# Attention block on one core: turned tiles kept in quarter order, two small tiles normalised on GpSimd, new orders

## The reference, cut to what matters

```python
# x: (4, 512, 256); H=16 heads of E=128, KV=4 key/value heads, G=4
xn = layernorm(x)
Q = (xn @ Wq + bq); K = (xn @ Wk + bk); V = (xn @ Wv + bv)
scores = einsum('blhe,bmhe->bhlm', Q, K) / sqrt(128)   # causal mask added
attn = softmax(scores)
ctx = einsum('bhlm,bmhe->blhe', attn, V)
y = gelu(ctx @ Wo + bo)
s = layernorm(xn + y) * gamma + beta
g = silu(ffn(xn))          # gate/up 256 -> 2x1024, silu(gate)*up, down to 256
out = x + s * g
```

## Time and profile before

| what | value |
|---|---|
| median of 3 runs | 708.92 us |
| the profiled execution, its own time | 708.16 us |
| span of the profiled execution | 706.4 us |
| mean granted TensorE clock | 0.956 |
| busy in the span: TensorE, VectorE, ScalarE, GpSimd | 89%, 71%, 60%, 36% |
| DMA: share of the 16 engines | 68.3% |
| data moved | 121.35 MB in 130870 packets |

### The profile page before, as it was taken

How to read it: one execution, slowest core, us unless ns; L and a number is a source line. 1 busy time by engine, 2 the same in 40 slices (tenths; PEclk the granted TensorE clock), 3 DMA queues, 4 the chain that set the end, 5 groups by cost and what they waited for, 6 DMA issues and landing times.

```text
span 706.4 us, 10602 instructions
## 1 busy us (share of the span) xinstructions
PE 625.7 (89%) x3342; PEld 532.6 (75%) x3342; DVE 503.5 (71%) x1119; ACT 421.4 (60%) x1023; POOL 255.9 (36%) x211
## 2 busy tenths in 40 slices
...
GB/s 254 139 82 30 61 89 59 31 1 113 222 177 204 233 198 227 194 214 170 247 163 208 235 205 242 194 196 190 238 193 237 197 203 232 187 208 225 201 143 30
DMA packets 130870, 121.35 MB, mean 172 GB/s; under 512 B 16256, under 2 KB 112640, under 8 KB 128768
## 3 DMA queue, kind: packets, MB, share of 16 engines
q1 hardware_dynamic: 130128, 120.37, 68.3%
...
q10 hardware_dynamic: 688, 0.33, 0.2%
...
## 4 chain that ended last, share of the span: by engine, by line
PE 41%; DMA 29%; DVE 10%; SPq 6%; ACT 6%; issue 4%; POOL 2%; DVEq 0%; ACTq 0%; POOLq 0%
PE bank L925 13%; DMA probs<-p_scratch 11%; DMA i_scratch<-inv 9%; DMA p_scratch<-probs 8%; PE down_ps L925 6%; PE down_ps L965 6%; PE bank L954 6%; PE bank L952 6%; SPq L455 5%; DVE probs L864 4%; PE down_ps L1039 4%; ACT probs L651 3%; DMA raw<-in_wgu 2%; POOL pT_lo L532 2%; ACT pT_hi L659 1%
## 5 line engine op out<-in xcount | busy, mean ns | idle before, releaser
L532 POOL TENSOR_TENSOR pT_lo<-probs,pT_hi 128x512 fp32r<-128x512 f32 x160 | 203.4, 1296 | 341.0 <-ACT pT_hi L659 340.4
L659 ACT ACTIVATE pT_hi<-probs 128x512 fp32r<-128x512 f32 x160 | 95.3, 624 | 120.3 <-DMA probs<-p_scratch 99.0
L651 ACT ACTIVATE probs<-probs,least 128x512 f32<-128x512 f32 (+3 forms) x256 | 140.4, 552 | 4.9 <-DVE least L851 4.9
L851 DVE CUSTOM_DVE_ANT_0 probs<-bank,mask 128x512 f32<-128x512 f32 (+3 forms) x256 | 115.7, 485 | 11.8 <-PE bank L925 10.9
L864 DVE STREAM_TRANSPOSE probs<-probs 128x2048 f32<-128x2048 f32 (+1 forms) x64 | 95.7, 1496 | 21.5 <-ACT probs L651 21.5
L925 PE MATMUL down_ps<-pT_lo,v_hi 128*128 128x512 f32 x160 | 69.5, 434 | 45.3 <-POOL pT_lo L532 45.1
L1039 PE MATMUL down_ps<-wo_lo,cT_hi 128*128 128x256 f32 x256 | 74.6, 291 | 10.4 <-DVE cT_lo L883 10.4
L878 DVE TENSOR_TENSOR down_ps<-down_ps,inv_b 128x512 f32<-128x512 f32 x64 | 68.8, 1075 | 16.9 <-DMA inv_b<-i_scratch 8.7
L870 DVE SCALAR_TENSOR_TENSOR qT_lo<-bank,bias,qT_hi 128x512 fp32r<-128x512 f32 x64 | 47.7, 746 | 44.9 <-ACT qT_hi L645 44.5
L925 PEld LDWEIGHTS down_ps<-pT_lo,v_hi 128*128 128x128 f32 x160 | 31.4, 196 | 61.4 <-POOL pT_lo L532 58.3
L1039 PE MATMUL down_ps<-wo_hi,cT_lo 128*128 128x256 f32 x256 | 73.0, 285 | 0.0
...
## 6 DMA issues: line engine op xcount, KB each, us to landing
p_scratch<-probs SPq DMA_DIRECT2D x16, 1024.0 KB, 5.2
...
```

Source lines behind the costliest of these rows:

```text
L532: nc.gpsimd.tensor_tensor(lo[:], turned(t)[:, j], f32(hi[:]), ALU.subtract).then_inc(probsT_split, 1)
L651: nc.scalar.activation(p, p, ACT.Exp, bias=least[:, u, g:g + 1], scale=-1.0, accum_out=total[:, n * T + t, g:g + 1]).then_inc(exp_done, 1)
L659: nc.scalar.activation(pT[(pair_no - 1) % PT_BUFFERS][0][:], turned(t)[:, j], ACT.Copy).then_inc(probsT_hi, 1)
L851: nc.vector.tensor_tensor_reduce(out=blocks_view(t)[:, g], in0=ps[:, 0:(t + 1) * P].rearrange("p (k i) -> p k i", i=BLOCK), in1=mask[:, (T ...
```

## The change

1. Keys in quarter order. For t > 0 the score product reads its keys as `(q j i)` and not as `(j q i)`: first the keys of quarter 0 of every block of 128, then quarter 1, and so on. A unit's turned tile is then read back in runs of (t+1)·512 bytes in place of 512 bytes, still with four DMAs of 32 partitions. `ph` and `pl` read four separate runs of 128 columns where they read 512 columns in a row. The mask has a copy for each tile (128x1280 in place of 128x512) and is loaded after the last weight is split.
2. For tiles 0 and 1 (`NORMED`) GpSimd multiplies the probabilities with the reciprocals in place (new steps `no0`, `no1`, 128x512 and 128x1024), before `tt`. Their `c`, `IW` and `IR` go. All four tiles still go through DRAM (`BY_DRAM`); the new code for tiles that don't (`T`, `pd`) is there but no tile uses it.
3. New orders on all engines and on SP.

```diff
 TENSOR_ORDER
-P3.2- S3.1 S3.2 S3.3 P3.3- O0-- P2.0- P2.1- S2.0 S2.1 S2.2 S2.3 P2.2- O3- S1.0 S1.1 S1.2 P1.0- S0.0 S0.1 S1.3
+P3.2- S3.2 S3.3 P3.3- O0-- P2.0- P2.1- S2.0 S2.1 S1.0 S1.1 P2.2- O3- S2.2 S2.3 P1.0- S1.2 S1.3 S0.0 P1.1- S0.1
...
 TRANSFER_ORDER
-W2- IR3- IW1- IW2- W1- R2- W0- IR2- R1- R0- W3 LX@3 IW0- IR1- IW3 ST--@0 IR0- R3
+IW2- ST--@1 W1- R2- W0- R1- LX@3 IR2- R0- IW3 W3 IR3 R3 W2
...
+BY_DRAM = (0, 1, 2, 3)
+NORMED = (0, 1)
+MASK_AT = [P * t * (t + 1) // 2 for t in range(T + 1)]
...
-        return p_scratch[i][t].rearrange("(a i) (j q) n -> q i j a n", a=BLOCKS, q=BLOCKS)[q]
+        return p_scratch[i][t].rearrange("(a m) (q n) -> q m a n", a=BLOCKS, q=BLOCKS)[q]
...
-                    sp.dma_start(turned(t)[q * BLOCK:(q + 1) * BLOCK].rearrange("p j (a n) -> p j a n", a=BLOCKS),
+                    sp.dma_start(probs[t][q * BLOCK:(q + 1) * BLOCK].rearrange("p (a n) -> p a n", a=BLOCKS),
                                  turned_back(n % 2, t, q)).then_inc(probsT_in[t], 16)
...
+        def normalised(n, t):
+            pool.wait_ge(inv_made, INVERTED["ri", n, t])
+            at = inv[:, n % KV * T + t, :]
+            if t in BY_DRAM:
+                p = by_blocks(t)
+                factor = at.rearrange("p (k g i) -> p k g i", k=1, i=1).to_broadcast([P, BLOCKS * (t + 1), G, BLOCK])
...
+            nc.gpsimd.tensor_tensor(p, p, factor, ALU.mult).then_inc(probs_made, 1)
...
                 elif kind == "tt":
                     t = step[2]
-                    dve.wait_ge(exp_done, max(EXPED["e", n, t, g] for g in range(G)))
-                    p = probs[t][:].rearrange("p k g i -> p (k g i)")
-                    nc.vector.transpose(p, p).then_inc(blocks_made, 1)
+                    if t in NORMED:
+                        dve.wait_ge(probs_made, NORMALISED["no", n, t])
+                    else:
+                        dve.wait_ge(exp_done, max(EXPED["e", n, t, g] for g in range(G)))
+                    nc.vector.transpose(probs[t][:], probs[t][:]).then_inc(blocks_made, 1)
...
             if t:
-                last = product(ps[:, 0:width], [w[:, t * P:(t + 1) * P] for w in qT[g]],
-                               [w[:, 0:width] for w in kT], True, True)
+                keys = [w[:, 0:width] for w in kT]
+                if t in BY_DRAM:
+                    keys = [w.rearrange("p (j q i) -> p q j i", q=BLOCKS, i=BLOCK) for w in keys]
+                last = product(ps[:, 0:width], [w[:, t * P:(t + 1) * P] for w in qT[g]], keys, True, True)
```

More of the change, by code:

```diff
@@ L234, in build @@
     v_s = pair("v", [P, T, KV * E])
-    probs = [sb(f"probs{t}", [P, BLOCKS * (t + 1), G, BLOCK]) for t in range(T)]
+    probs = [sb(f"probs{t}", [P, G * (t + 1) * P]) for t in range(T)]
+    mask = sb("mask", [P, MASK_AT[T]])
     pT = [pair(f"pT{i}", [P, G * P]) for i in range(PT_BUFFERS)]
```

148 lines of the change are left out of this document (103 added, 45 removed).

## The result

The changed kernel took 649.25 us (median of 4 runs, 648.0 to 651.28), the kernel before 710.59 us on the same chip (4 runs, 708.58 to 713.49). The ratio is 0.914 (95% interval 0.909 to 0.918): 61 us, or 8.6%, faster. The forecast was 674 us with a range of 656 to 697, so the direction was right and the size was not: the forecast was 25 us too high, and the time lies outside the range. The profiled run took 651.28 us with a span of 649.5 us and a mean granted clock of 0.978 (before 0.956).

The account below looks back on a forecast made before the run. A loop of tile writes and reads through DRAM, not TensorE, was taken to set the 32.04 us period; at 29.5 + 0.4 = 29.9, 2.14 x 16 = 34.2 us come off 708.2, giving 674 us, range 656 to 697.

Parts of the forecast that it names:

- Turn 0: The one period in four that includes the V matmuls: TensorE's own work sets it, 26.7 + 5.5 = 32.2 us.
- The new loop: Tile 3's write and read, tile 2's write and read, back to tile 3's write: 28.6 us, from 31.55.
- Landing to W3: From tile 2's read-back landing to issue of the next tile 3 write: 6.4 us, same instructions in the same order.
- R2 to landing: From issue of tile 2's read-back from DRAM to its landing: 6.4 us, unchanged at an unchanged rate.
- W3 to R3: From issue of tile 3's write to DRAM to issue of its read-back: 5.3 us in place of 6.44, 1.1 saved.
- R3 to R2: From issue of tile 3's read-back to issue of tile 2's: 10.5 us in place of 12.33, through less surrounding traffic.
- For `pl3.0` I add 0.4 us a period: GpSimd's two normalising steps ahead of pl3.0, which TensorE waits for: 0.4 us a period charged, ends 0 and 3.7.
- the drain: End of the program: taken as the same kind of chain, its saving counted within the 16 periods at 2.14 us each.
- the fast rival: Wider rows read at 393 GB/s, loop 23.9 us, TensorE alone decides: period 29.5, 667 us, down to 656; chance 0.17.
- Half comes back: GpSimd's normalising waits on the reciprocals, pl3.0 late by 1 to 1.5 us: period 31, 691 us; chance 0.17.
- the wait only moves: The DRAM loop is cut, but another loop through probs3 takes over at 32 us: 708 us; chance 0.08.
- W1 blocks SP: Tile 1's later write holds up tile 2's read in SP's queue: period 33, 724 us; chance 0.08 shared with slower key reading.

Follow-up runs that it names:

- N alone: The kernel before, its engine orders and key order kept, with only tiles 0 and 1 normalised on GpSimd (their c, IW and IR gone): 678.55 us, ratio 0.955.

## Why the forecast was wrong, step by step

- **The cause was right.** Opening the loop through DRAM gives 641 us (before) and 637 us (after), and a delay put into it is paid. Turn 0, which TensorE limits, was to be 32.2 and is 32.4.
- **Failed: "The new loop: 5.3 + 10.5 + 6.4 + 6.4 = 28.6 us. Turns 1 to 3 take 28.6".** They take 27.34 on average, by the second table 4.77 + 10.65 + 6.05 + 5.86. Over twelve turns that is 15 us, the largest part of what the forecast missed. Term by term:
  - *Landing to W3, 6.4.* The forecast has `ph2.0`, `ph2.1`, `e3.1` to `e3.3` and `tt3` "in the same order". It missed that `e3.0` stood between `ph2.0` and `ph2.1` and has been moved ahead of them. Before, R2 landed at 479.54 and `tt3` began at 483.57; the first row below is that `e3.0`. In the other two, of the changed kernel, `ph2.0` and `ph2.1` follow each other and `tt3` starts 3.4 us after the landing in place of 4.0. The segment is 5.79 us in most turns, 6.37 in most turns before.

```profile
480.10 0.70 ACT L651 ACTIVATE probs<-probs,least 128x512 f32<-128x512 f32 x1
...
449.23 1.15 ACT L698 ACTIVATE pT_hi<-probs 128x512 fp32r<-128x512 f32 x2 [1.43 <-DMA probs<-p_scratch]
...
452.63 2.28 DVE L915 STREAM_TRANSPOSE probs<-probs 128x2048 f32<-128x2048 f32 x1
```

  - *R2 to landing, 6.4, "unchanged at an unchanged rate".* The rate is unchanged, but the four DMAs are issued 0.6 us sooner: 6.05.
  - *W3 to R3, 5.3.* It was sized by 5.2 us for W3's landing; the median is 4.4 now.
  - *R3 to R2, 10.5.* It came out (10.65) with some luck. In the changed kernel W2 waits 1.7 us for `tt2` once R3 is issued (0.1 before), which the forecast did not have. It lands 7.10 us after its issue, where it took 9.27 before.
- **Failed: "For `pl3.0` I add 0.4 us a period."** Without any normalising the time is the same (649.17 and 649.25), and the two steps are shorter than the rows they were sized by: the form 128x1024 took 1.90 us and 128x512 1.04, forecast 2.41 and 1.30.

```profile
L567 POOL TENSOR_TENSOR probs<-probs,inv 128x1024 f32<-128x1024 f32 x16 | 30.3, 1896 | 123.8 <-DVE inv L908 123.8
L567 POOL TENSOR_TENSOR probs<-probs,inv 128x512 f32<-128x512 f32 x16 | 16.7, 1042 | 17.4 <-DVE inv L908 17.2
```

  Over the 15 intervals 0.4 each are 6 us. With the 15 above that makes 21; the forecast saved 2.14 x 15 = 32.1 us there and the profiled runs show 50.8, so 18.7 were missing. The two agree but for the base: the 15 intervals of before average 31.7 and not 32.04, and three of 15 have a `V`, not one in four.
- **Mis-sized: the drain.** "I count it with the 16 periods", so 2.1 us. It became 7.4 us shorter, 5.3 us more. Most of it is in one place: in the last period W3 to R3, where LX and the small transfers stood, fell from 9.80 to 5.58 us. 18.7 + 5.3 - 1.3 (the start) = 22.7 us, which is what the forecast missed between the profiled runs (56.9 us saved in place of 34.2); the changed kernel's median lies 2.0 us below its profiled run, and that makes the 25.
- **Failed, though not in the sum: "A stretch in which TensorE never idled gives what can really be had: ... 28.1 without `V` and 29.5 with its share."** This floor gave the fast rival's period, and the lower end of the range was reached from there. The stretch, 537.08 to 598.82 in the kernel before, followed a stall of 3.96 us, and its first part ran at half the clock (a row of TensorE's timeline, then two stretches):

```profile
537.08 0.80 PE L925 MATMUL down_ps<-pT_lo,v_hi 128*128 128x512 f32 x1 [3.96 <-POOL pT_lo L532]
...
537.08:542.00 4.92, 4.92 (x12) 3.90 (x13) 2.85 (x4) 3.88 (x9) 3.71 (x3) 0.50 0.72 160
560.00:598.82 38.82, 38.81 (x210) 33.21 (x208) 34.91 (x83) 29.15 (x71) 15.18 (x11) 1.00 0.89 212
```

  The clock column is 0.50 (the 1.2 GHz level) in the second row and 1.00 (2.4 GHz) in the third. Some 2.5 us of the 61.74 were the price of the stall before it, counted as TensorE's own pace. The forecast had the right number one paragraph earlier: the work at the pace of the chain, 26.7 us and 32.2 with `V`, where the changed kernel without the trip shows 26.77 and 32.23. That is a mean of 28.1, and the rival's own sum would then give 708.2 - 3.9 x 16 = 646 us in place of 667. The stalls of the earlier trace rows cost twice: 55.5 us of idle time and, behind them, slower matmuls. By the mean clock over the periods, (1 - 0.96) x 524 = 21 us of TensorE's time were lost before and (1 - 0.99) x 467 = 5 now, and TensorE's busy time fell by those 16 us.
- **Mis-sized: normalising.** "VectorE loses two `c` ... which it doesn't feel except as slack" holds nearly: 4 us. What went with them was more than "saved 1.1" for W3 to R3, where 2.0 us were measured (6.68 to 4.69) for all parts together: N alone is 32 us in the old orders, and three quarters of what it is worth in the new ones (1.6 of 2.1%) came with the small transfers. The chain had it in one line, `i_scratch<-inv` with 9%, and the forecast did not read the chain by line. Two 2 KB writes and two 256 KB reads in a strict queue cost by what waits behind them, not by their bytes.
- **Right, and yet mis-priced: wider rows.** The rate is as forecast: 218 to 236 GB/s into 32 partitions at any length of run (the trace of before had 197; why it was lower there is open). The Trainium skill (SBUF — State Buffer, section Door 1: the DMA port swizzle) has 32 neighbouring partitions on 8 of 16 ports; the runs agree that the partitions decide. The Trainium skill's 189 GB/s in the same section were measured on transfers of 1 MiB, with about 218 as the limit of larger ones; 218 to 236 were measured here, inside a set. But the forecast equated "no faster" with "worth nothing". SP issues each DMA of the wide form in 0.43 us in place of 0.64, and the quarter order brought 1.9% (13 to 16 us) in the new orders and 1.8% in the old.
- **Right: nothing for the reading of keys and for the mask.** The first score matmul of three took 403 ns at 512 columns (396 before) and 348 at 384 columns (339), and with the trip taken out a turn of TensorE is 26.77 us in the new key order and 26.70 in the old:

```profile
L982 PE MATMUL bank<-kT_lo,qT_hi 128*128 128x512 f32 x64 | 25.8, 403 | 1.6 <-DVE qT_lo L921 1.5
L982 PE MATMUL bank<-kT_lo,qT_hi 128*128 128x384 f32 x64 | 22.3, 348 | 3.3 <-DVE least L900 3.3
```

- **The rivals.** "Wider rows are faster" had the better time (667, down to 656) for a reason that the rate refutes. "Half comes back", "the wait only moves" and "W1 blocks SP" didn't occur: `P` waits for 5.9 us in all, 2.1 at most, and R2 was issued 0.02 us after W2 had landed in every turn without `V`, so W1 never held it.
- **Open.** How the gain of the orders divides between their parts (R3 nearer to W3, W2 behind R3, `e3.0` and `nm` moved) was not tried part by part, nor was what sets SP's issuing time.
